# Four-layer GNN kernel on one core: the edge-attribute product as eight 32-row products into four PSUM banks

## The reference, cut to what matters

```python
# layer 1 (sum)
msg = jax.nn.relu(x[src] + edge_attr @ We + be)
aggr = jax.ops.segment_sum(msg, dst, num_segments=x.shape[0])
# layer 2, twice (maximum)
msg = x[src] @ W_msg + edge_attr @ W_edge
agg = jax.ops.segment_max(msg, dst, num_segments=x.shape[0])
return agg + x @ W_root + b
```

## Time and profile before

| what | value |
|---|---|
| runs | 13138.51, 13133.17, 13126.07 us; median 13133.17 |
| profiled execution, first to last instruction | 13179.5 us (no time of its own is listed beside this span; it lies 46.3 us, 0.35%, above the median) |
| mean granted TensorE clock | 0.541 |
| PE busy | 4527.1 us (34%), 15877 matmul rows |
| PEld busy | 3022.1 us (23%) |
| DVE busy | 6535.8 us (50%) |
| ACT busy | 1994.5 us (15%) |
| POOL busy | 8151.7 us (62%) |
| DMA | 1264.02 MB, mean 96 GB/s |
| gathers of e1, e2a, e2b | 3 x 1616, first to last start 2257.1, 2253.5, 2256.3 us |

### The profile page before, as it was taken

How to read it: one execution, slowest core, us unless ns; L and a number is a source line. 1 busy time by engine, 2 the same in 40 slices (tenths; PEclk the granted TensorE clock), 3 DMA queues, 4 the chain that set the end, 5 groups by cost and what they waited for, 6 DMA issues and landing times. The chain is left out here.

```text
span 13179.5 us, 81573 instructions
## 1 busy us (share of the span) xinstructions
PE 4527.1 (34%) x15877; PEld 3022.1 (23%) x15877; DVE 6535.8 (50%) x10237; ACT 1994.5 (15%) x4360; POOL 8151.7 (62%) x8551
## 2 busy tenths in 40 slices
PE   3354455555222222232222222222222234434443
PEld 3244344444110111111111111111111123333332
DVE  9543344444544454454445455444544544444445
ACT  3233333333100000010000000000000022222223
POOL 1455555555676666656666666766666666666665
PEclk7555555555555555555555555555555555555555
DMA  2355555555333333323333332333333222222222
GB/s 76 106 155 154 149 152 155 153 159 152 99 86 82 87 89 87 88 72 85 87 87 93 81 91 79 87 85 88 89 87 86 81 58 66 69 68 68 68 69 63
DMA packets 1007936, 1264.02 MB, mean 96 GB/s; under 512 B 483123, under 2 KB 740467, under 8 KB 1007331
## 3 DMA queue, kind: packets, MB, share of 16 engines
q0 software_dynamic: 303696, 520.91, 17.5%
q1 hardware_dynamic: 638139, 635.93, 14.8%
q10 hardware_dynamic: 65600, 101.96, 2.7%
HBM read 829.46 MB, written 428.44 MB: 95 GB/s over the span
## 5 line engine op out<-in xcount | busy, mean ns | idle before, releaser
L789 POOL DMA_INDIRECT e_got<-kv_tab,dst_cols x1661 | 1574.5, 948 | 1281.7 <-DVE e_pay L894 770.2
L1843 POOL DMA_INDIRECT e_got<-h_tab,src_tcols x1612 | 1540.9, 956 | 881.8 <-issue 473.8
L1151 POOL DMA_INDIRECT e2a_got<-x_tab,src_cols x1616 | 1531.3, 948 | 775.7 <-issue 556.2
L1151 POOL DMA_INDIRECT e_got<-x_tab,src_cols x1616 | 1553.5, 961 | 718.3 <-issue 586.9
L1151 POOL DMA_INDIRECT e2b_got<-x_tab,src_cols x1616 | 1531.3, 948 | 745.7 <-issue 518.8
L1168 PE MATMUL e2b_EA<-we_W_edge,e2b_attr 128*128 128x384 f32 x808 | 574.9, 866 | 1331.2 <-DVE e2b_emsg L1187 728.3
L1168 PE MATMUL e_EA<-we_We,e_attr 128*128 128x384 f32 x808 | 578.3, 871 | 1297.8 <-issue 898.1
L1168 PE MATMUL e2a_EA<-we_W_edge,e2a_attr 128*128 128x384 f32 x808 | 572.0, 862 | 1300.4 <-issue 767.3
L894 DVE TENSOR_TENSOR e_pay<-e_got,e_Q 128x384 f32<-128x384 f32 x416 | 230.2, 553 | 1570.4 <-ACT e_Q L962 1129.1
L1940 DVE TENSOR_TENSOR_SCAN e_run<-e_Z,e_run,e_msg 98x512 f32<-98x512 f32 x404 | 516.9, 1279 | 795.4 <-ACT e_msg L2005 619.8
L805 PE MATMUL e_Q<-e_window,e_pick 128*128 128x96 f32 x3328 | 758.9, 408 | 79.1 <-issue 41.2
(11 more groups left out here) (373 smaller groups left out, 10316.0 us busy)
## 6 DMA issues: line engine op xcount, KB each, us to landing
scan_out<-e_out SPq DMA_DIRECT2D x416, 200.0 KB
e_window<-q_tab SPq DMA_DIRECT2D x1664, 48.0 KB
scan_out<-e_out SPq DMA_DIRECT2D x404, 196.0 KB
scan_out<-e_out SPq DMA_DIRECT2D x202, 384.0 KB
scan_out<-e2a_out SPq DMA_DIRECT2D x202, 384.0 KB
scan_out<-e2b_out SPq DMA_DIRECT2D x202, 384.0 KB
e_rel<-rel_row ACTq DMA_DIRECT2D x208, 256.0 KB
e_keep<-keep_row ACTq DMA_DIRECT2D x208, 200.0 KB
```

What stands on the lines that cost most here:

```text
L789: e.indirect_dma_start(got[i][:, k, :], None, kv_tab, bass.IndirectOffsetOnAxis(dst_c[:, c * K + k:c * K + k + 1], axis=0)).then_inc(s_g[i ...
L1151: e.indirect_dma_start(got[s % RS][:, k, :], None, x_tab, bass.IndirectOffsetOnAxis(src_cols[:, q:q + 1], axis=0)).then_inc(edge_got[s % R ...
L1843: e.indirect_dma_start(got[c % RG][:, k, :], None, h_tab, bass.IndirectOffsetOnAxis(src_tcols[:, q:q + 1], axis=0)).then_inc(s_g[c % RG], 16)
```

## The change

The attribute product of a step is made as eight matmuls in place of two: for each half h and each of the four groups k one product of 32 rows (partitions 32k to 32k + 31 of the attribute tile and of the weight tile) by 96 columns. Group k goes into bank k, half h into columns 96h to 96h + 95 of it. The product tile `EA` is now 128 by 4 by 512, four banks, and there is one of it instead of two of two banks; so PE waits for the add of step s - 1 before the products of step s, where it waited for that of step s - 2. The root product goes into columns 192 and up of bank 0. The weight tiles are 128 by 96, the 32 by 96 weight four times one under the other, and need no clearing. The edges of a step are numbered (k h) in place of (h k), in `attr_S` and in the access patterns of the add, so that each group's two halves lie side by side.

```diff
--- before.py
+++ after.py
@@ -194,7 +194,7 @@
         Wyi, Wrc = keepb("Wyi", [D, 2 * D]), keepb("Wrc", [D, D])
         w96 = {n: keepb("w_" + n, [D, D]) for n in
                ("qW", "kW", "vW", "W1", "W2", "W1_msg", "W1_root", "W2_msg", "W2_root", "W")}
-        we = {n: keepb("we_" + n, [P, K * D]) for n in ("We", "W1_edge", "W2_edge")}
+        we = {n: keepb("we_" + n, [P, D]) for n in ("We", "W1_edge", "W2_edge")}
         cols = {n: keepb("c_" + n, [D, 1]) for n in ("b1", "b2", "gamma", "beta")}
         rows = {n: keepb("r_" + n, [P, D]) for n in ("be", "l2b1", "l2b2", "bias")}
         att = keepb("att", [D, 2])
@@ -345,7 +345,7 @@
                 loads.append((att[:, n:n + 1], t[key].rearrange("(n a) -> n a", a=1)))
             for n, key in (("We", "L1_gnn_We"), ("W1_edge", "L2_gnn_W1_edge"), ("W2_edge", "L2_gnn_W2_edge")):
                 for k in range(K):
-                    loads.append((we[n][k * DE:(k + 1) * DE, k * D:(k + 1) * D], t[key]))
+                    loads.append((we[n][k * DE:(k + 1) * DE, :], t[key]))
 
             def pairs(buf, lo, n, y):
                 v = buf[:, lo:lo + n].rearrange("p (b h y) -> p b h y", h=2, y=y)
@@ -373,7 +373,6 @@
                     for j in range(6):
                         e.dma_start(scan_out[EP + j * CHS:EP + (j + 1) * CHS, :], zero[:, 0:D]).then_inc(s_z, 16)
                     e.dma_start(scan_out3[EP:EP + 1, :], zero[0:1, :]).then_inc(s_z, 16)
-                    e.wait_ge(p_set, 1 + len(we))
                     for dst, src in loads:
                         e.dma_start(dst, src).then_inc(s_w, 16)
                     e.wait_ge(s_w, 16 * len(loads))
@@ -407,8 +406,6 @@
                     e.wait_ge(p_node, 4)
                     e.tensor_scalar(node_q[:, :], node_q[:, :], 0.5, None, ALU.add).then_inc(p_node, 1)
                     e.memset(zero[:, :], 0.0).then_inc(p_set, 1)
-                    for n in we:
-                        e.memset(we[n][:, :], 0.0).then_inc(p_set, 1)
                     e.memset(mean_m[:, :], 1.0 / D)
                     e.memset(eps_col[:, :], EPS).then_inc(p_mat, 1)
                     e.memset(src_cols[:, NCH * K:], 0).then_inc(p_mat, 1)
@@ -1088,7 +1085,8 @@
                 emsg = [ph.sb(f"emsg{i}", [P, 2 * K, D]) for i in range(3)]
                 run = [ph.sb(f"run{i}", [P, 3, W2]) for i in range(3)]
                 out = [ph.sb(f"out{i}", [P, 2 * K, D]) for i in range(3)]
-                EA = [ph.ps(f"EA{i}", [P, 2, CH]) for i in range(2)]
+                EA = ph.ps("EA", [P, K, CH])
+                ROOT = EA[:, 0, 2 * D:2 * D + P]
                 F = [ph.ps(f"F{i}", [P, 2 * CH]) for i in range(2)]
                 t_root, root_done = ph.sem("t_q"), ph.sem("v_pick")
                 EVERY = NS // NT
@@ -1156,16 +1154,18 @@
                     def _(e):
                         for s in range(NS):
                             e.wait_ge(s_attr[s % RA], 16 * (s // RA + 1))
-                            after(e, v_add, s - 1)
+                            after(e, v_add, s)
                             q = root_tile(s)
                             if q is not None:
                                 after(e, root_done, q)
                                 if root:
-                                    e.matmul(EA[s % 2][:, 0, K * D:K * D + D], xT_all[:, q * P:(q + 1) * P], root_w[:, :], start=True, stop=True).then_inc(t_root, 1)
+                                    e.matmul(ROOT[:, 0:D], xT_all[:, q * P:(q + 1) * P], root_w[:, :], start=True, stop=True).then_inc(t_root, 1)
                                 else:
-                                    e.transpose(EA[s % 2][0:D, 0, K * D:K * D + P], X[:, q, :], ident[:, :]).then_inc(t_root, 1)
+                                    e.transpose(ROOT[0:D, :], X[:, q, :], ident[:, :]).then_inc(t_root, 1)
                             for h in range(2):
-                                ins = e.matmul(EA[s % 2][:, h, 0:K * D], attr[s % RA][:, h * P:(h + 1) * P], edge_w[:, :], start=True, stop=True)
+                                for k in range(K):
+                                    at = slice(k * DE, (k + 1) * DE)
+                                    ins = e.matmul(EA[:, k, h * D:(h + 1) * D], attr[s % RA][at, h * P:(h + 1) * P], edge_w[at, :], start=True, stop=True)
                             ins.then_inc(t_attr, 1)
 
                     @block.vector
@@ -1178,14 +1178,14 @@
                             if q is not None:
                                 e.wait_ge(t_root, q + 1)
                                 if root is None:
-                                    e.tensor_copy(xT_all[:, q * P:(q + 1) * P], EA[s % 2][0:D, 0, K * D:K * D + P]).then_inc(root_done, 1)
+                                    e.tensor_copy(xT_all[:, q * P:(q + 1) * P], ROOT[0:D, :]).then_inc(root_done, 1)
                                 elif root_scale is None:
-                                    e.tensor_tensor(R[:, q, :], EA[s % 2][:, 0, K * D:K * D + D], root_bias[:, :], ALU.add).then_inc(root_done, 1)
+                                    e.tensor_tensor(R[:, q, :], ROOT[:, 0:D], root_bias[:, :], ALU.add).then_inc(root_done, 1)
                                 else:
-                                    e.scalar_tensor_tensor(R[:, q, :], EA[s % 2][:, 0, K * D:K * D + D], root_scale[:, q:q + 1], root_bias[:, :],
+                                    e.scalar_tensor_tensor(R[:, q, :], ROOT[:, 0:D], root_scale[:, q:q + 1], root_bias[:, :],
                                                            ALU.mult, ALU.add).then_inc(root_done, 1)
-                            e.tensor_tensor(emsg[s % 3][:, :, :].rearrange("p (h k) d -> p h (k d)", h=2), EA[s % 2][:, :, 0:K * D],
-                                            got[s % RS][:, :, :].rearrange("p (h k) d -> p h (k d)", h=2), ALU.add).then_inc(v_add, 1)
+                            e.tensor_tensor(emsg[s % 3][:, :, :].rearrange("p (k h) d -> p k (h d)", h=2), EA[:, :, 0:2 * D],
+                                            got[s % RS][:, :, :].rearrange("p (k h) d -> p k (h d)", h=2), ALU.add).then_inc(v_add, 1)
 
                         def forward(s):
                             e.wait_ge(a_relu if relu else v_add, s + 1)
@@ -2214,7 +2214,7 @@
 
     attr_pad = np.zeros((n_padded, DE), attr.dtype)
     attr_pad[:n_edges] = attr
-    attr_S = np.ascontiguousarray(attr_pad.reshape(4, NCH // 2, P // 4, 2, K, DE).transpose(1, 4, 5, 3, 0, 2).reshape(NCH // 2, K * DE, 2 * P))
+    attr_S = np.ascontiguousarray(attr_pad.reshape(4, NCH // 2, P // 4, K, 2, DE).transpose(1, 3, 5, 4, 0, 2).reshape(NCH // 2, K * DE, 2 * P))
     arrays = {"x": x_pad, "src_cols": src_cols, "src_tcols": tile_cols(src_pad),
               "dst_pad": dst_pad, "dst_prev": dst_prev, "attr_S": attr_S,
               "sort_src": in_rows(src, np.arange(n_nodes, dtype=src.dtype)), "sort_dst": in_rows(dst, np.full(n_nodes, n_nodes, dst.dtype))}
```

## The result

| | runs, us | median | against before in the same session |
|---|---|---|---|
| before | 13138.51, 13133.17, 13126.07, 13150.62 | 13135.84 | |
| with the change | 13400.7, 13376.7, 13391.94, 13372.02 | 13384.32 | 1.0184 (1.0171 to 1.0196) |

The change makes the kernel slower by 1.84%, 248 us by the medians. (Ratios and their 95% intervals stand here as recorded; the quotient of two medians can differ a little, here it is 1.0189.) The forecast was 14,350, that is 9% slower: the sign is right, the size is five times too large. Two later sessions gave 1.0193 (1.0171 to 1.0214) and 1.0239 (1.0218 to 1.0259).

What follows compares the result with a forecast made beforehand. It took each step to be bound by the late count of the product's matmuls. 1.97 us times 606 steps (1194) plus 25 for root steps made +1219 us: 14,350 us against 13,133.17, range 12,350 to 19,000.

Steps and rivals of the forecast that it cites:

- the prediction's example: Step 67 of a gather pass: t_attr's count arrives 18.4 us after the matmul end that PE's row shows.
- the 16 rows a step: Sign on PE: the changed product's MATMUL rows come at 16 a step.
- SP's load beside the add: Sign on SP: its attribute load still goes out beside the add, both waiting for the product's count.
- the three memsets: POOL's preparation loses three memsets of 0.407 us, then waits 12.76 us for ACT anyway: nothing.
- the shape of the add: DVE's add, still 768 elements a partition, now read from four banks: 0.95 us stays.
- What the late signal costs: Step path of add, POOL's restart, eight gathers and late signals: 13.15 us against 11.18, 1194 us over 606 steps.
- the term of 1.97 us a step: Extra time a step, 13.15 against 11.18 us, times 606 steps: 1194 us.
- a pause after every eight gathers: Sign on POOL: it ends a step's eight gathers, pauses 2 to 4 us and goes on after the add.
- low end, 12.3 us: Lower bound of a step: add 0.96, PE start 0.1, signal 11.2 us as now but unhidden; 13,850 us in all.
- count-bound: Rival: 2.8 us a pair holds whatever POOL does, 44.8 us a step, 34,300 us; 0.22 with halfway forms.
- Two product tiles let PE be two steps ahead: Kernel before, PE: being two steps ahead keeps 18 us of lateness to a cost of 1.18 us a step.
- law of 2.8 us a pair: Product's count on PE: each MATMUL and LDWEIGHTS pair takes 2.8 us, so four pairs make 11.2 us a step.

Runs made afterwards that it cites:

- e0: Not a run: the kernel's stage ahead of e1, unchanged in name; first to last gather 2884.3 us before, 2860.4 us with the change.
- single_late: Kernel before, but PE waits for the add of step s - 1, not s - 2: 13147.52 us, 1.0002; in the 11,238 us session 1.0001.
- drain8: Kernel before, with POOL waiting before every eighth step's gathers until all adds so far are done: 13133.19 us, 0.9997.
- eight_single: Kernel before with eight products of 96 columns on 128 rows, and PE waiting for the add of step s - 1: 13403.04 us, 1.0206.
- eight_late: Kernel before with eight products of 96 columns on all 128 rows in place of two: 13324.7 us, 1.0123; in the 11,238 us session 1.0.
- dve24: Kernel before with DVE's add of a step made as 24 adds of 32 columns: 13259.38 us, 1.0072.
- fewer: Kernel before with one product in place of two, one scan in place of three, attributes of two steps in one load: 13106.42 us, 0.9967.
- act24: Kernel before with 24 small copies a step on ScalarE in 404 steps, for which nothing waits: 13723.59 us, 1.0441.

## Why the prediction was wrong

**Right:** where the add waits long, it waits for the product's completion and not for its matmuls; that comes some 20 us after them (18.4 us in the prediction's example, 20.8 in the changed kernel's); the 16 rows a step; SP's load beside the add; the three memsets cost nothing (e0's first gather starts at 439.1 us, before at 439.5), nor does the shape of the add (0.944 us on average, before 0.951).

**Wrong: the step "What the late signal costs".** It said: "add 0.96, POOL restarts 0.27 later (8964.68), eight gathers 7 x 1.25 + 0.94 = 9.69, signals 2.23 after: 13.15 us a step". It laid the late signal end to end with the gathers in every step, as a path of 13.15 us. Measured are 11.54, so the term of 1.97 us a step is 0.36 in e2b and 0.40 on average. The lateness is no latency that each step has to pay: the add waited for it in 65 of 202 steps, 855.1 us in all, and POOL gathered for three steps on end and then halted once, where the forecast had a pause after every eight gathers. After a halt of POOL the next two steps are prompt or nearly so (the loads at 8968.21 and 8976.08 come 0.4 and 3.2 us after their products' end, the one at 8999.23 is stuck again). What fits is that completions are let out at a limited rate and pile up behind it. Then the average counts, and most changes of the path leave it as it was: a tighter wait with few rows (single_late, 1.0002), a forced halt (drain8, 0.9997), two or four gather buffers (1.0177 and 1.0211 for the changed kernel's 1.0184 to 1.0239). One doesn't: with sixteen pairs a step the tighter wait costs some 70 us (eight_single), and a rate alone doesn't say why; that stays open. The forecast's own low end, 12.3 us, had the same flaw.

That the sign is right is in part luck. Of the 252 us of eight_single 178 come from the number of rows, for which the forecast's sum has no term: it held the product hidden and charged the path alone, and the tighter wait costs no more than the 74.

**What stands in its place: the rows.** In place of most of the path the term is the number of rows. By the passes' lengths, 24 more rows a step cost 0.32 us on PE (eight_late, 13 ns each), 23 more cost 0.20 on DVE (dve24, 9 ns each if all of it is the rows'), and 6.5 fewer give 0.10 us ('fewer', 15 ns each by the same reading). The change's 24 with the tighter wait cost 0.40 (243 / 606). The rival "count-bound" at 2.8 us a pair read the right quantity with the wrong law: the 11.20 us a step in drain8 agree with it for four pairs, but with sixteen a step would take 44.8 us, and it takes 11.54.

**The sentence that should have been doubted:** "Two product tiles let PE be two steps ahead, which is why 18 us of lateness cost only 1.18 us a step." It was the main ground for charging the single tile, and single_late refutes it for four pairs a step: with PE one step ahead the kernel takes the same time. The sign for a rate was in the trace: the steps of the earlier trace rows are 11.2 and 11.9 us, and most others in e2b are multiples of 0.7 us too, closer than a chain over four engines and a gather's landing would keep. But the prediction's law of 2.8 us a pair rested on few steps: over the whole of e2b they run from 4.3 to 16.8 us, and about a third are 11.2.

**What lets the completions out** is not shown. What is: every engine is affected (PE, DVE in dve24, ACT in act24, POOL in 'fewer', SP's mask issues of 4.48 us); instructions come at multiples of 0.7 us in the stretches shown; and where they are late most semaphore changes are missing from the trace. The Trainium skill (NOTIFIC — the notification-queue block, "7.1 Overflow: three behaviours, one of which stalls the engine") says that the block which writes the trace's records always holds back its producers rather than lose one inside, and that a stall count there would mean that "the notification path had throttled an engine"; the Trainium skill (the same page, "10. Constraints, capacities, measured rates") puts some 500 records in flight inside it. That would fit most of the above: rows, not work, cost; a pile that fills, then clears in a halt. It doesn't explain the missing changes, since by that page nothing is lost inside the block. The Trainium skill, in that section, also has it measured that emitting a record costs an engine nothing, which the prompt session bears out ('eight', 1.0) and the late ones don't. It stays an argument: no run here was made without records, and every time in this document is of an execution with them. So it is open whether the 1.84% would be there at all in an execution that nobody records.

## What to carry to other kernels

When semaphores change long after the instructions that count them, look for a rate before you add up a path: count how often a wait ends late, change a wait or a buffer count, and if the time doesn't move, count instructions. Measure a change in two sessions, and compare with the kernel before in the same one, since 11,238 and 13,144 us were the same kernel on the same chip. And a matmul made three times as fast is worth nothing where the product was hidden, while its rows may have a price.

## What was not expected of the hardware

- The same kernel on the same chip took 11,238 us in one session and 13,144 in a later one; the gathers of a pass took 2,256 us in a late one and 2,017 in the prompt one (there by the profile of 'single', which took as long as the kernel before).
- In late sessions an instruction of 0.1 us can come every 0.7 or 1.4 us (dve24, the rows shown), and ACT's copies every 1.21 us during a pass and every 0.10 us after it (act24).
- Sixteen matmul rows of 32 rows by 96 columns into four banks took 1.19 us, sixteen of 128 rows by 96 took 3.70 (PE's ends are modelled).
- In 'fewer', where the other engines have fewer rows, some gathers stretch from 0.94 to 1.85 us, and the mean from 0.948 to 1.067.
